# Seven block products instead of eight for y and the scores, in an fp32r graph attention kernel

## The reference

```
q = x Wq^T,  k = x Wk^T,  v = x Wv^T
rel = adj^T * (q k^T)                  # elementwise with the 0/1 matrix
rel = rel / norm(rel, axis=2)          # each row by its length
out = layernorm(x + rel v)             # over the last axis
```

## Time and profile before

| | us |
|---|---|
| median of 3 runs (2122.88 to 2123.11) | 2122.96 |
| span of the profiled execution, first to last instruction | 2121.3 |
| what lies around the span, against the median | 1.7 |
| PE busy | 2106.8 (99%) |
| DVE, ACT, POOL busy | 1029.7, 525.7, 404.8 |
| DMA moved | 108.2 MB, 51 GB/s |

### The profile page before, as it was taken

The page is one execution under the profiler, slowest core; times in us unless marked ns, Lnnn a source line. Parts: engine busy times, 40 slices in busy tenths (PEclk is TensorE's granted clock), DMA queues, the critical chain, the costliest instruction groups (busy, mean ns, idle before and its releaser), DMA issues.

```text
span 2121.3 us, 26238 instructions
## 1 busy us (share of the span) xinstructions
PE 2106.8 (99%) x9264; PEld 1739.0 (82%) x9264; DVE 1029.7 (49%) x2160; ACT 525.7 (25%) x913; POOL 404.8 (19%) x389
## 2 busy tenths in 40 slices
PE   8999999999999999999999999999999999999998
PEld 7888888888888888888888888888888888888887
DVE  4453544535445354453544545445454554545445
ACT  4222212222122221122212222122222222222121
POOL 0221202212022120221212112121221212212122
PEclk9999999999999999999999999999999999999999
DMA  6011110111101111011111101112011120111101
GB/s 218 15 56 50 59 59 15 59 44 59 59 20 54 44 59 59 28 52 38 59 59 40 60 19 59 59 40 79 3 57 59 40 79 5 59 54 40 59 11 50
DMA packets 55998, 108.20 MB, mean 51 GB/s; under 512 B 3248, under 2 KB 3248, under 8 KB 55984
## 3 DMA queue, kind: packets, MB, share of 16 engines
q1 hardware_dynamic: 55984, 108.02, 14.1%
HBM read 74.45 MB, written 33.55 MB: 51 GB/s over the span
## 4 chain that ended last, share of the span: by engine, by line
PE 96%; issue 2%; DVE 1%; POOL 0%; DMA 0%; ACT 0%; DVEq 0%; ACTq 0%; SPq 0%; POOLq 0%
PE ring L236 22%; PE ring L238 22%; PE ring L237 22%; PE score L238 10%; PE score L237 10%; PE score L236 10%; DVE rel_lo L465 1%; DVE x_lo L431 1%; PE score L264 0%; PE score L265 0%; PE score L266 0%; DMA adj_sb<-wk 0%; POOL rstd L584 0%; DVE masked L479 0%; DVE rel_lo L446 0%
## 5 line engine op out<-in xcount | busy, mean ns | idle before, releaser
L574 POOL TENSOR_TENSOR square_sum<-square_sum,squares 128x512 f32<-128x512 f32 x224 | 302.3, 1349 | 801.3 <-ACT squares L400 801.3
L236 PE MATMUL score<-y_hi,x_hi 128*128 128x512 f32 x1024 | 398.3, 389 | 0.0
L237 PE MATMUL score<-y_lo,x_hi 128*128 128x512 f32 x1024 | 398.3, 389 | 0.0
L236 PE MATMUL ring<-v_hi,rel_hi 128*128 128x512 f32 x1024 | 398.3, 389 | 0.0
L237 PE MATMUL ring<-v_lo,rel_hi 128*128 128x512 f32 x1024 | 398.3, 389 | 0.0
L238 PE MATMUL ring<-v_hi,rel_lo 128*128 128x512 f32 x1024 | 398.3, 389 | 0.0
L238 PE MATMUL score<-y_hi,x_lo 128*128 128x512 f32 x1024 | 398.3, 389 | 0.0
L388 ACT ACTIVATE rel_hi<-masked 128x512 fp32r<-128x512 f32 x256 | 161.9, 632 | 758.9 <-DVE masked L479 758.9
L479 DVE TENSOR_TENSOR masked<-score,adj_sb 128x512 f32<-128x512 f32 x256 | 177.0, 691 | 317.5 <-PE score L238 317.0
L237 PEld LDWEIGHTS ring<-v_lo,rel_hi 128*128 128x128 f32 x1024 | 192.2, 188 | 40.0
L236 PEld LDWEIGHTS ring<-v_hi,rel_hi 128*128 128x128 f32 x1024 | 192.2, 188 | 39.9
(11 more groups left out here) (43 smaller groups left out, 2023.4 us busy)
## 6 DMA issues: line engine op xcount, KB each, us to landing
x_raw<-xT SPq DMA_DIRECT2D x32, 1024.0 KB, 5.3
res<-x SPq DMA_DIRECT2D x32, 1024.0 KB, 5.2
out<-res SPq DMA_DIRECT2D x128, 256.0 KB, 2.0
adj_sb<-adj SPq DMA_DIRECT2D x2, 2048.0 KB, 11.0
adj_sb<-wq SPq DMA_DIRECT2D x4, 256.0 KB, 3.9
adj_sb<-wk SPq DMA_DIRECT2D x4, 256.0 KB, 4.6
adj_sb<-wvT SPq DMA_DIRECT2D x1, 1024.0 KB, 9.6
```

Of the source, the lines that this page charges most:

```text
L236: pe.matmul(bank_ap, l_hi, r_hi, start=(i == 0), stop=False)
L237: pe.matmul(bank_ap, l_hi, r_lo, start=False, stop=False)
L574: pool.tensor_tensor(square_sum[:, :], square_sum[:, :], squares[:, i % SQRING, :], ALU.add).then_inc(square_added, 1)
```

## The change

The scores x·(a x^T) are made in two Strassen-like stages (the form with seven products and fifteen sums). x^T is cut in four blocks of 256x512, X11 to X22, and `a` in four of 256x256; sums of blocks (S1 to S4 of x, T1 to T4 of a) are formed and split once, and y's four blocks come from seven block products instead of eight. The same seven left factors are used again for the scores, with sums T1 to T4 of y's blocks. A batch is now:

- y: 7 rounds of 2 products of 6 matmuls (`y_products`; the order is `Y_ROUNDS`), 84 matmuls;
- scores: 4 row tiles per block, in two pairs; per pair 7 rounds of 2 products of 6 matmuls (`s_products`, `S_ROUNDS`), 84 a pair, 168 in all;
- v: 8 groups of 12 (`v_products`), 96; outputs: 8 tiles of 24, 192.

So 540 matmuls a batch. The stages follow one another, no stage of another half or batch lies between them. Products accumulate in PSUM where the form allows it (P1 is copied out and P2 added on top of it); the other sums are made by DVE from PSUM and SBUF, T1 and T4 of y (and their lo parts) by POOL, the masking of one block by POOL.

`rel` is held whole in fp32 (`rel`, 128 x 8 x 1024) and split by columns just before each output tile (`chunk`: 1024 elements a partition, three slots). Norms of both halves are made in the v stage, behind the 5th and the 6th lo part of v on DVE. The adjacency no longer stays in SBUF: eight DMAs of 512 KB a batch into slots that it shares with x's raw blocks. `a` (7 blocks, hi and lo, 3.67 MB) and `wv` (2.1 MB) share one buffer: both are written to DRAM at the start (`a_kept`, `w_kept`) and read back each batch. Sums of x blocks are made by POOL during the outputs. All of the split of `a`, `wv` and x comes before the first product of the first batch.

The diff, cut to what is spoken of:

```diff
+B11, B21, B22, T1, T2, T3, T4 = range(7)
+LEFT = {1: X11, 2: X12, 3: S4, 4: X22, 5: S1, 6: S2, 7: S3}
+RIGHT = {1: B11, 2: B21, 3: B22, 4: T4, 5: T1, 6: T2, 7: T3}
+Y_ROUNDS = (1, 5, 2, 6, 4, 7, 3)
+S_ROUNDS = (1, 6, 2, 7, 5, 4, 3)
+X_PIECES = (X22, X21, X11, X12, S1, S3, S2, S4)
+X_SUMS = (S1, S3, S2, S4)
...
+        def v_bank(m):
+            return bank[(2 + m) % 8]
...
+            load_adj(2)
+            load_adj(3)
+            for t in range(RRING):
+                load_res(0, t)
+            sp.wait_ge(wv_split, KD)
+            sp.dma_start(w_kept, wv_split_stage.bitcast(F32)).then_inc(w_stored, DMA)
+            sp.wait_ge(a_split, 7)
+            sp.dma_start(a_kept, aw[:, :].bitcast(F32)).then_inc(a_stored, DMA)
+            sp.wait_ge(w_stored, DMA)
...
+                sp.wait_ge(y_done, b * Y_COUNT + Y_COUNT)
+                sp.dma_start(aw[:, 0:8 * BANK].bitcast(F32), w_kept).then_inc(w_loaded, DMA)
+                sp.wait_ge(s_m12, b * HT + 1)
+                load_adj(6)
+                sp.wait_ge(s_m12, b * HT + 2)
+                load_adj(7)
...
+            def y_products(b):
+                pe.wait_ge(a_loaded, b * DMA + DMA)
+                for k in Y_ROUNDS:
+                    left, right = LEFT[k], RIGHT[k]
...
+                        if k == 6:
+                            pe.wait_ge(o_taken, b * MT + (4 + j + 1))
+                        if k == 2:
+                            pe.wait_ge(y_p1, b * 2 + (j + 1))
+                        if k == 4:
+                            pe.wait_ge(y_w, b * 2 + (j + 1))
+                        if k == 7:
+                            pe.wait_ge(y_q, b * 2 + (j + 1))
+                        if k == 3:
+                            pe.wait_ge(y_c11, b * 2 + (j + 1))
+                            pe.wait_ge(y_split[B11], b * 2 + (j + 1))
+                        product(y_bank[y_into[k]][j][:],
+                                [((a_hi[:, right, d, cols(j)], a_lo[:, right, d, cols(j)]),
+                                  (x_hi[:, left, d, :], x_lo[:, left, d, :])) for d in range(2)],
+                                k in (1, 5, 6, 3)).then_inc(y_done, 1)
...
+            def s_products(b, pair):
+                for k in S_ROUNDS:
+                    left, right = LEFT[k], RIGHT[k]
+                    if pair == 0:
+                        pe.wait_ge(y_split[right], b * 2 + 2)
+                    for i in (2 * pair, 2 * pair + 1):
+                        j = i % 2
...
+                        if k == 5 and pair == 0:
+                            pe.wait_ge(y_split[T3], b * 2 + (j + 1))
+                        if k == 5 and pair == 1:
+                            pe.wait_ge(s_c21, b * HT + (j + 1))
+                        if k == 2:
+                            pe.wait_ge(s_p1, b * HT + (i + 1))
+                        if k == 7:
+                            pe.wait_ge(s_u2, b * HT + (i + 1))
+                        if k == 4:
+                            pe.wait_ge(s_r, b * HT + (i + 1))
+                        if k == 3:
+                            pe.wait_ge(s_c22, b * HT + (i + 1))
...
+            def v_products(b):
+                pe.wait_ge(w_loaded, b * DMA + DMA)
...
+            def outputs(b):
+                for t in range(MT):
+                    c = t % CRING
+                    if t < 2:
+                        pe.wait_ge(v_split, b * MT + (7 + t))
+                    pe.wait_ge(chunk_split, b * MT + (t + 1))
...
+            def y_blocks(b):
+                for j in range(2):
+                    act.wait_ge(y_done, y_count(b, 1, j))
+                    act.activation(y_p1_raw[j], y_bank["a"][j][:], ACT.Copy).then_inc(y_p1, 1)
+                for j in range(2):
+                    act.wait_ge(y_done, y_count(b, 2, j))
+                    act.activation(y_c11_raw[j], y_bank["a"][j][:], ACT.Copy).then_inc(y_c11, 1)
+                    y_hi_piece(b, B11, j, y_bank["a"][j][:])
+                for j in range(2):
+                    act.wait_ge(y_done, y_count(b, 4, j))
+                    y_hi_piece(b, T3, j, y_bank["b"][j][:])
+                for j in range(2):
+                    act.wait_ge(y_t2, b * 2 + (j + 1))
+                    y_hi_piece(b, T2, j, y_t2_raw[j])
+                for j in range(2):
+                    act.wait_ge(y_c22, b * 2 + (j + 1))
+                    y_hi_piece(b, B22, j, y_b22_raw[j])
+                for j in range(2):
+                    act.wait_ge(y_t1, b * 2 + (j + 1))
+                    y_hi_piece(b, T1, j, y_t1_raw[j])
+                    act.wait_ge(y_c12, b * 2 + (j + 1))
+                    y_hi_piece(b, B21, j, y_b21_raw[j])
+                for j in range(2):
+                    act.wait_ge(y_t4, b * 2 + (j + 1))
+                    y_hi_piece(b, T4, j, y_t4_raw[j])
+            def s_copy(b, i):
+                act.wait_ge(s_done, s_count(b, 1, i))
+                act.activation(c21(i), s_bank[i // 2]["a"][i % 2][:], ACT.Copy).then_inc(s_p1, 1)
...
+                y_blocks(b)
+                s_copy(b, 0)
+                s_copy(b, 1)
+                for name, i in square_order[0:6]:
+                    square(b, name, i)
+                s_copy(b, 2)
+                s_copy(b, 3)
+                for name, i in square_order[6:]:
+                    square(b, name, i)
+                for m in range(MT):
+                    v_piece(b, m)
+                    if 1 <= m <= CRING:
+                        chunk(b, m - 1)
...
+            def y_blocks(b):
+                a, bb, c = y_bank["a"], y_bank["b"], y_bank["c"]
+                for j in range(2):
+                    dve.wait_ge(y_p1, b * 2 + (j + 1))
+                    dve.wait_ge(y_done, y_count(b, 5, j))
+                    dve.tensor_tensor(y_b22_raw[j], bb[j][:], y_p1_raw[j], ALU.add).then_inc(y_w, 1)
+                for j in range(2):
+                    y_lo_piece(b, B11, j, a[j][:])
+                for j in range(2):
+                    dve.wait_ge(y_w, b * 2 + (j + 1))
+                    dve.wait_ge(y_done, y_count(b, 6, j))
+                    dve.tensor_tensor(y_b21_raw[j], c[j][:], y_b22_raw[j], ALU.add).then_inc(y_q, 1)
+                for j in range(2):
+                    dve.wait_ge(y_c11, b * 2 + (j + 1))
+                    dve.wait_ge(y_hi_made[T3], b * 2 + (j + 1))
+                    dve.tensor_tensor(y_t2_raw[j], bb[j][:], y_c11_raw[j], ALU.add).then_inc(y_t2, 1)
+                    y_lo_piece(b, T3, j, bb[j][:])
+                for j in range(2):
+                    y_lo_piece(b, T2, j, y_t2_raw[j])
+                for j in range(2):
+                    dve.wait_ge(y_done, y_count(b, 7, j))
+                    dve.tensor_tensor(y_b22_raw[j], c[j][:], y_b22_raw[j], ALU.add).then_inc(y_c22, 1)
+                for j in range(2):
+                    y_lo_piece(b, B22, j, y_b22_raw[j])
+                for j in range(2):
+                    dve.wait_ge(y_q, b * 2 + (j + 1))
+                    dve.wait_ge(y_done, y_count(b, 3, j))
+                    dve.tensor_tensor(y_b21_raw[j], a[j][:], y_b21_raw[j], ALU.add).then_inc(y_c12, 1)
+                for j in range(2):
+                    y_lo_piece(b, B21, j, y_b21_raw[j])
...
+                s_blocks(b, 0)
+                s_blocks(b, 1)
+                for m in range(MT):
+                    v_piece(b, m)
+                    if 1 <= m <= CRING:
+                        chunk(b, m - 1)
+                    if m in (4, 5):
+                        norms(b, m - 4)
...
+                    output(b, t)
+                    if t + CRING < MT:
+                        chunk(b, t + CRING)
+                    normalise(b, t)
...
+            def t1_raw(b, j):
+                pool.wait_ge(y_t2, b * 2 + (j + 1))
+                pool.wait_ge(y_c22, b * 2 + (j + 1))
+                pool.tensor_tensor(y_t1_raw[j], y_b22_raw[j], y_t2_raw[j], ALU.subtract).then_inc(y_t1, 1)
+            def t4_raw(b, j):
+                pool.wait_ge(y_c12, b * 2 + (j + 1))
+                pool.tensor_tensor(y_t4_raw[j], y_b21_raw[j], y_t2_raw[j], ALU.subtract).then_inc(y_t4, 1)
+            def y_lo_piece(b, q, j, source):
+                pool.wait_ge(y_hi_made[q], b * 2 + (j + 1))
+                pool.tensor_tensor(y_lo[:, q, j, :], source, y_hi[:, q, j, :].bitcast(F32),
+                                   ALU.subtract).then_inc(y_split[q], 1)
+            def y_blocks(b):
+                t1_raw(b, 0)
+                t1_raw(b, 1)
+                y_lo_piece(b, T1, 0, y_t1_raw[0])
+                t4_raw(b, 0)
+                y_lo_piece(b, T1, 1, y_t1_raw[1])
+                t4_raw(b, 1)
+                y_lo_piece(b, T4, 0, y_t4_raw[0])
+                y_lo_piece(b, T4, 1, y_t4_raw[1])
...
+            def mask22(b, i):
+                pool.wait_ge(adj_loaded[HT + i], b * DMA + DMA)
+                pool.wait_ge(s_c22, b * HT + (i + 1))
```

(61 more changed lines are left out.)

698 lines of the change are left out of this document (401 added, 297 removed).

## The result

The changed kernel takes **2207.9 us** (2205.76 to 2208.08), against 2122.9 before: the ratio is 1.040, with an interval of 1.038 to 1.041. It is slower by 4.0%, where 0.6% was forecast.

What follows compares the result with a forecast made beforehand. PE's matmul count times 0.2267 us spacing bounds the kernel. A batch of 122.4 + 3.7 + 4.2 + 0.3 = 130.6 us, sixteen 2089.6, plus start 38.0, tail 6.1 and 1.7 gave 2135.4 us, 0.6% slower; range 2107 to 2175.

Steps and rivals of the forecast that it cites:

- both edges: Stage transitions y to scores and v to outputs, where PE was forecast to stall 3.7 and 4.2 us a batch.
- POOL's six instructions, L: Y-to-scores edge: time of six POOL instructions ahead of ACT's copy, taken as 9.2 us, bounds 7.74 and 10.8.
- score pause: Y-to-scores edge: PE's third score round waits for ACT's copy of P1, 3.7 us a batch.
- output pause: V-to-outputs edge: first output waits for v's seventh lo part behind two norm passes on DVE, 4.2 us a batch.
- first y product: Start: everything is split first, so the first y product comes at 32 to 34 us.
- This is sure as far as the rate of PE stays: Saving claim: fewer matmuls at unchanged 0.2267 us spacing save 8.6 us a batch, 137 us in all.
- PE's counted start: Time at which the first batch counts as begun: 35.5 to 39.5, taken as 38.0 us, 18.4 later than before.
- The mechanism: Rival: PE restarts at half rate after each of 32 stalls, 2 us each, +64, 2199 us; chance 0.12.
- The stalls are shorter than 6.5 us, which speaks against: Argument against the half-rate rival, comparing stalls with the 6.5 us without matmuls at the start; rival's chance 0.12.
- part of the stalls restarting slow: Part of the range's upper end, 2175 us, together with L at 10.8 and start at 39.5.
- the wait for the written weights: Start: ACT and DVE wait for w_kept's write, 2.1 MB, 7 to 11 us, before their first y step.
- The DMA rival: Rival: a streamed transfer comes late at the batch's start, 1 us a batch, 2151 us; chance 0.10.

Runs made afterwards that it cites:

- the kernel with both edits: Changed kernel with the second norm pass behind v's eighth lo part on DVE and P1's copies ahead of T4's hi parts on ACT: 2053.9 us, ratio 0.968.
- the copy was out of the way, the 4.1 us one and one of 1.2 us: Changed kernel with ACT's copies of P1 moved ahead of T4's hi parts: 2126.3 us, ratio 1.002.
- the pauses ordered away: Kernel with early norms, ACT's copy moved and DVE reordered, plus first score sums ahead of B22's lo parts and POOL's x sums after DVE's a sums: 2009.9 us.
- the 4.1 us one and one of 1.3 us: Changed kernel with POOL's T4 sums ahead of T1's lo parts, ACT's order kept: 2132.1 us, ratio 1.005.
- the 3.4 us one and one of 1.1 us: Changed kernel with the second half's norms behind v's eighth lo part instead of the sixth: 2106.7 us, ratio 0.993.
- 3.46 us in the kernel before: Kernel before, with PE made to wait for the last output tile's normalisation ahead of the first v group in 15 batches: 2197.0 us.
- the first of the two start timelines above: Changed kernel with ACT's copy moved, c12 and B21's lo parts ahead of B22's on DVE, norms behind v's second and fourth lo parts: 2021.9 us, ratio 0.953.
- the second: Kernel with the norms early, plus POOL's x sums after DVE's a sums and first score sums ahead of B22's lo parts: 2009.9 us, ratio 0.947.

## Why the prediction was wrong

**What held.** The matmuls: 8688, at 0.2267 us while the clock is up. The walk of both edges:

| step | forecast | measured |
|---|---|---|
| y's start to POOL's first sum | 17.60 | 17.73 (582.30 to 600.03) |
| POOL's six instructions, L | 9.2 | 9.31 (to 609.34) |
| from there to PE | 1.36 | 1.20 (to 610.54) |
| score pause | 3.7 | 3.39 |
| output pause | 4.2 | 4.08 |
| first y product | 32 to 34 | 39.54 |

The chain in the trace, POOL, then ACT:

```profile
600.03 2.99 POOL L797 TENSOR_TENSOR rel<-rel 128x512 f32<-128x512 f32 x2 [14.89 <-DVE rel L643]
602.99 1.74 POOL L806 TENSOR_TENSOR yv<-rel,yv 128x512 fp32r<-128x512 f32 x1
604.69 1.29 POOL L802 TENSOR_TENSOR rel<-rel 128x512 f32<-128x512 f32 x1
605.94 1.73 POOL L806 TENSOR_TENSOR yv<-rel,yv 128x512 fp32r<-128x512 f32 x1
607.63 1.71 POOL L802 TENSOR_TENSOR rel<-rel 128x512 f32<-128x512 f32 x1
609.37 0.63 ACT L490 ACTIVATE yv<-rel 128x512 fp32r<-128x512 f32 x1 [2.73 <-POOL rel L802]
609.91 1.07 ACT L520 ACTIVATE rel<-bank 128x512 f32<-128x512 f32 x2
```

POOL's six instructions stand in the order forecast; the sixth ends at 609.34, and ACT's hi part and the two copies follow at once. And DVE before the outputs:

```profile
659.71 0.70 DVE L708 STREAM_TRANSPOSE squares<-square_sum 128x512 f32<-128x512 f32 x1
...
664.38 0.69 DVE L696 TENSOR_TENSOR yv<-bank,yv 128x512 fp32r<-128x512 f32 x1
664.99 0.70 DVE L708 STREAM_TRANSPOSE squares<-square_sum 128x512 f32<-128x512 f32 x1
...
669.77 1.29 DVE L696 TENSOR_TENSOR yv<-bank,yv 128x512 fp32r<-128x512 f32 x2
670.51 0.50 PE L339 MATMUL bank<-yv 128*128 128x512 f32 x1 [3.92 <-DVE yv L696]
```

The norm passes keep their 4.7 us each (the earlier trace rows had 4.75), the seventh lo part of v comes only behind the second, and PE starts at 670.51.

**What failed.** The sentence was "This is sure as far as the rate of PE stays", and the sum then used one spacing for all 540 matmuls. The term left at zero is the clock behind a pause: a restart was given 0.15 us and nothing for the half rate. Without it a batch would have been 122.4 + 3.4 + 4.1 + 0.3 = 130.2 us (forecast 130.6); the mean of fifteen batches is (2088.72 - 66.13) / 15 = 134.84 (two matmuls at the same place of the first and of the last batch). The 4.6 us between them are 74 us over 16 batches; the forecast missed 72.5, since it had the pauses together 0.4 us a batch too long (6 us) and the start 3.5 us too short (1.5 us in PE's counted start, 2.0 us of slow spacings behind it). The mechanism stood among the rivals, with the place, 2 us a pause, 2199 us and a chance of 0.12; measured were 2.1 us a pause on average, (81.8 - 13.2) / 32, where 13.2 us is the sum of slow spacings in the kernel with both edits, whose 31 short pauses don't lower the clock; and 2207.9 us. What was wrong is its weight. "The stalls are shorter than 6.5 us, which speaks against" was no argument: the rows before held just one long idle stretch, at the start, so they bounded the length from one side only, and the earlier trace rows did show what a start at half rate looks like. The page of the Trainium skill that was named there (TensorE: Matmul & The Clock Gate, HAM oscillation — how this bites in real kernels) has it right that pauses between bursts bring the lower clock back, and the runs agree; that our bursts were long, some 50 us, was the wrong reason to set it aside, since each pause counts by itself.

**The range** reached 2175 by "part of the stalls restarting slow". All 32 did.

**Smaller misses.** The first y product came 5.5 us later than my upper end. I gave POOL's x sums 2 us of effect on DVE; three of DVE's sums of `a` took 2.1 us more each, and x's lo parts more too. It cost little, since the wait for the written weights had been counted too long (7 to 11 us; the write took 6.3 and hid behind PE's first two rounds): PE's counted start was 39.5 us against 38.0. The row at 14.70 that the forecast took for x's second MB is the landing of the weights of v; in the changed kernel ACT starts on x's second load at 14.35, so nothing came of it. L came out at 9.31 with POOL's share of the contention sized right from two rows, but DVE's was not: its two-input lo parts, put at 0.87 us each beside POOL, took 1.5 and 1.7. So B21's lo parts, forecast for 23, came at 608.2 - 582.3 = 25.9, hidden behind the copy; they became the pause of 1.2 us as soon as the copy was out of the way. The DMA rival is refuted: 265 MB move in place of 108, and PE doesn't wait for them once.

**Where the gain went.** 137 us were to be had and 85 were lost, 222 us in all. Of these the pauses took 119.5, the low clock about 69 more, the start 20, the restarts and the small wait before the second score round most of the remaining 13. With the pauses ordered away, 2009.9 us stand 113 us under the kernel before: of 137 only the longer start is missing (41.5 against 19.64 us, and its slow restart of 2.4).

**Open.** The price of a pause isn't a constant: 2.1 us in the changed kernel with two long ones a batch, 1.4 with the 4.1 us one and one of 1.2 us, 1.6 with the 4.1 us one and one of 1.3 us, 1.0 with the 3.4 us one and one of 1.1 us (there six of the sixteen long ones were free), 1.4 with 3.46 us in the kernel before. It comes in steps: where the clock falls, either 6 to 8 spacings behind the pause are over 0.4 us or 12 to 14, and in the changed kernel batches of the one and of the other kind alternate: 1.5 to 1.8 us a pause, then 2.9 to 3.0 (restart included). What decides it, beside the length, the runs don't settle.

## What to carry to other kernels

Where a kernel is bound by PE and runs without a gap, a rewrite that saves matmuls must be judged by the gaps it opens, and each gap must be priced at its length and at the half-rate matmuls behind it: 0.4 us on average for a pause of 2.25 us, 1.0 to 2.1 us for 3.4 to 4.1 us. Look for what stands in the queues in front of the one instruction that PE needs: here changes of order on ACT, DVE and POOL, with no work removed, turned 4% slower into 5% faster. Move an instruction away from POOL's long ones only after looking at what takes its place beside them.

## What the runs showed of the hardware

A DVE instruction with two SBUF inputs doesn't share with a POOL instruction over 1024 elements, by these spans it waits for it: 2.83 us in place of 0.69 for 512 elements, while POOL's instruction takes 2.60 to 3.21 us. POOL's end at 23.25 and 25.99 in the first of the two start timelines above, DVE's about 0.55 us behind each, at 23.80 and 26.55. In the second, four of POOL's cost the seven lo parts 8.6 us, 2.15 each. Before, with a POOL instruction of 1.3 us, showed DVE at 0.87. In the y stage of the changed kernel two pairs of such DVE instructions took 2.99 and 3.35 us in place of 1.29, while a pair with one input from PSUM (L650), also beside POOL, kept 1.28:

```profile
598.00 1.29 DVE L615 TENSOR_TENSOR yv<-rel,yv 128x512 fp32r<-128x512 f32 x2
...
600.59 2.99 DVE L615 TENSOR_TENSOR yv<-rel,yv 128x512 fp32r<-128x512 f32 x2
603.50 1.28 DVE L650 TENSOR_TENSOR rel<-bank,rel 128x512 f32<-128x512 f32 x2
604.87 3.35 DVE L615 TENSOR_TENSOR yv<-rel,yv 128x512 fp32r<-128x512 f32 x2
```

An instruction with one SBUF tensor seems to be held as well. DVE's normalisation, 0.55 us otherwise, took 2.62 us in the kernel with both edits while POOL made a sum of x; no experiment took the two apart. Part of the 502 us that DVE is busy longer in the changed kernel is waiting of these kinds; how much was not summed. The two normalisations:

```profile
137.98 0.55 DVE L740 TENSOR_SCALAR res<-res,mean_var,rstd 128x512 f32<-128x512 f32 x1 [2.81 <-POOL rstd L850]
...
144.60 2.62 DVE L740 TENSOR_SCALAR res<-res,mean_var,rstd 128x512 f32<-128x512 f32 x1 [0.46 <-POOL rstd L850]
144.54 2.40 POOL L791 TENSOR_TENSOR scr<-scr 128x1024 f32<-128x1024 f32 x1
```
